# Dense experts of three batches as one chain of 13 tiles, two scan states on the partitions, another stage order

## The chip, the cores and the metric

The kernel runs on one core of one Trainium2 chip, in float32 throughout. The metric is device time in microseconds (us), as the median of several executions; a profile is taken of one further execution. The five engines are TensorE (PE in the rows, its weight loads PEld), VectorE (DVE), ScalarE (ACT), GpSimd (POOL) and SyncE (SP), which only issues transfers.

## The reference, cut to what matters

```python
x = L0_attn_x                                            # 4 batches x 512 tokens x 256 features
x = x + attention(layernorm(x))                          # per token, 16 heads against one key and value
x = x + dense_ffn(layernorm(x))                          # 2 experts, each token takes the likelier (argmax)
    g, u = x @ w_gate[e].T, x @ w_up[e].T                # 1024 wide
    y = (silu(g) * u) @ w_down[e].T * top_w
x = x + state_space(layernorm(x))                        # 8 states for each of 256 features
    x_dbl = x @ W_xproj.T                                # 32 ranks, B (8 states), C (8 states)
    delta = softplus(x_dbl[..., :32] @ W_dt.T + b_dt)
    h[t] = exp(delta * A) * h[t - 1] + (delta * x) * B   # along the 512 tokens
    y = sum over states of h * C, + x * D_param
x = x + sparse_ffn(layernorm(x))                         # top 6 of 64 experts, capacity 64, and a shared expert
```

## The kernel before, in words

Each of the four batches passes through attention, dense experts, the state-space scan and the gate of the sparse experts; then a tail runs all 32 pairs of sparse experts and sums their rows. P is 128, J = 4 tiles of 128 tokens make a batch, K = 2 blocks of 128 features make a row.

What each engine does is cut into stages, such as `ffn.1.3` (batch 1, step 3). One written list, `plan`, gives their order; each engine runs through it (`run`) and executes its own part of those stages that it has a part in, in that order. Nothing overtakes on an engine. Semaphores order the engines among themselves.

**Dense experts.** `route_gate` and `route_slots` norm the tokens, compare the two experts and number the tokens: those of expert 0 from the front, those of expert 1 from the back of 640 slots, so that five tiles (S0 = J + 1) hold a batch whatever the split, each tile of one expert only. GpSimd scatters the rows to `sorted_dram[b]`; SyncE loads them (`ffn_load`), TensorE turns them (`ffn_in`), and each tile takes two halves of 512 (`ffn`: two products of 512 columns for gate and two for up; tanh on ScalarE; `silu` on VectorE; `ffn_h`: four turned blocks) and `ffn_down`. A float32 product appears as two records. `ffn_out` stores the tiles, gathers the rows in token order and adds them. Four batches make 20 tiles, 40 halves.

**Scan.** `ssm_norm`, `ssm_in`, `ssm_proj` give x_dbl, with B and C stored to `bc_dram` and broadcast to all partitions as `bc` (16 rows of 512, 4 MB). `ssm_exp` and `ssm_delta` compute delta; while they run SyncE also issues four clears of `part_rows` (768 KB each, SyncE's `ssm_exp`). A batch has 8 groups: group g holds one block of 128 features on the partitions and two states side by side. For each, ScalarE makes two exponentials (`ssm_a`, line 966), VectorE multiplies (line 1217), scans (line 1221) and multiplies (line 1224), and TensorE adds the two states into `ssm_ps` with the identity (`ssm_sum`, line 728). `ssm_out` turns and adds the result.

**After it.** `gates_in`, `gates`, `places` and `rounds` choose the experts of a batch, `shared_mm`, `shared` and `shared_out` compute the shared expert. These stages of a batch lie among the scan of the next one.

**The start.** The first turn (`attn_turn.0`) waits for all five loads of attention weights, the gate row `g_row` the last of them.

Of the kernel before, what the change touches and what calls it, by code (L numbers as in the profile page):

```python
# [20 lines left out]
F32 = mybir.dt.float32  # L21
# [17 lines left out]
STEPS = S0 * HALF  # L39
# [4 lines left out]
PER_CHUNK = GROUPS // K  # L44
HS_RING = 3
# [23 lines left out]
RT_SEL, RT_DIFF, RT = J + 1, J + 2, J + 11  # L69
# [45 lines left out]
def build(nc, x, wq_t, bq, wkv_t, bkv, gate0, wg0_t, wu0_t, wd0_t, wx_t, wdt_t, b_dt, a_log, d_par,  # L115
          gate1_t, wgu1, wd1, shg_t, shu_t, shd_t, out):
    with ExitStack() as ctx:
# [17 lines left out]
        tile_thr = sb("tile_thr", [1, S0])  # L135
        slot_no = sb("slot_no", [E, CAP])
# [36 lines left out]
        a_col = sb("a_col", [P, K, NS])  # L173
# [23 lines left out]
        rt_ex = sb("rt_ex", [1, B, S0], I32)  # L197
        slot_idx = sb("slot_idx", [P, B, J], U32)
# [15 lines left out]
        bc = sb("bc", [P, 2 * NS, L])  # L214
# [28 lines left out]
        area = bc[:].rearrange("p n l -> p (n l)")  # L243
        at = [0]

        def carve(n):
# [26 lines left out]
        sorted_dram = [nc.dram_tensor(f"sorted_dram{b}", (SLOTS, D), F32).ap() for b in range(B)]  # L273
        ysorted_dram = nc.dram_tensor("ysorted_dram", (SLOTS, D), F32).ap()
# [6 lines left out]
        x_loaded = [sem(f"x_loaded{b}") for b in range(B)]  # L281
        w_attn_loaded = sem("w_attn_loaded")
# [7 lines left out]
        sorted_clear = [sem(f"sorted_clear{b}") for b in range(B)]  # L290
# [27 lines left out]
        du_ready = sem("du_ready")  # L318
        diag_ready = sem("diag_ready")
# [45 lines left out]
            attn_in.0 attn_turn.0 attn_qkv.0.0 attn_in.1 attn_in.2 attn_qkv.0.1 attn_qkv.0.2 ffn_load.0 attn_qkv.0.3  # L365
            attn_score.0 attn_turn.1 attn_add.0 route_gate.0 attn_qkv.1.0 attn_qkv.1.1 attn_qkv.1.2 route_slots.0
            attn_qkv.1.3 attn_score.1 attn_turn.2 attn_add.1 attn_qkv.2.0 ffn_in.0 attn_qkv.2.1 attn_qkv.2.2
            route_gate.1 attn_in.3 attn_qkv.2.3 route_slots.1 ffn.0.0 ffn.0.1 ffn_h.0.0 attn_score.2 ffn.0.2
            ffn_h.0.1 ffn.0.3 ffn_down.0.0 ffn_h.0.2 attn_turn.3 attn_add.2 attn_qkv.3.0 attn_qkv.3.1 route_gate.2
            attn_qkv.3.2 attn_qkv.3.3 ffn.0.4 ffn_h.0.3 route_slots.2 attn_score.3 ffn.0.5 ffn_down.0.1 ffn_h.0.4  # L370
            ffn.0.6 attn_add.3 ffn_h.0.5 ffn.0.7 ffn_down.0.2 ffn_h.0.6 route_gate.3 ffn.0.8 route_slots.3 ffn_h.0.7
# [47 lines left out]
        def run(eng, stages, skips=()):  # L419
# [3 lines left out]
            for name, batch, s in order:  # L423
                for ring, uses, mine in skips:
                    if name not in mine and name in uses:
                        ring.next(uses[name])
# [995 lines left out]
```

## Time and profile before

| | us |
|---|---|
| median of 3 runs | 717.83 (717.29 to 720.01) |
| the profiled execution | 719.09 |
| its span, first to last instruction | 717.4 |
| TensorE busy | 595.6 (83%) |
| VectorE busy | 512.9 (71%) |
| ScalarE busy | 198.1 (28%) |
| GpSimd busy | 104.7 (15%) |
| mean granted TensorE clock | 0.91 of full speed |

A share of the span is a mean over stages with different limits; the rows below cut the span into stages. The profiled execution took 1.7 us more than its span and 1.3 us more than the median.

### The profile page before, as it was taken

Reading aid. Unit: us, or ns where it says so; the run is one execution under the profiler, and the core shown is the slowest. Engines: PE = TensorE matmul, PEld = TensorE weight load, DVE = VectorE, ACT = ScalarE, POOL = GpSimd, SP = SyncE. Lnnn points to the kernel's source line nnn. Section 1 sums busy time; section 2 is a strip of 40 time slices with the busy share of each in tenths; the row PEclk is TensorE's granted clock in tenths of the full one; section 3 lists DMA queues with packets and bytes.
Section 4 is the critical chain, followed back from the end, with each engine's and each line's share of the span. In section 5 each row is a group of like instructions: output and inputs, shape, how many; then the busy total and the mean of one; then the engine's idle time right before and its main releaser. Section 6 shows DMA issues by size and latency. Waiting matters only on the chain.

```text
span 717.4 us, 7176 instructions
## 1 busy us (share of the span) xinstructions
PE 595.6 (83%) x2225; PEld 327.3 (46%) x2225; DVE 512.9 (71%) x1100; ACT 198.1 (28%) x387; POOL 104.7 (15%) x119
## 2 busy tenths in 40 slices
PE   4359998879998869998889988887656699999875
PEld 3235555525555446554355643553243244444554
DVE  7967966155995859997579998699985545555364
ACT  1112221226332334431543232521301133332000
POOL 2022021200002000002000010000000446664200
PEclk9757998998999959999899999999875899999999
DMA  7940000309202192011471010997004579998497
GB/s 276 399 147 32 1 31 15 118 2 359 89 0 67 32 375 80 0 38 30 175 236 37 1 52 16 348 352 230 0 1 164 176 249 364 363 370 294 152 415 290
DMA packets 50371, 114.35 MB, mean 159 GB/s; under 512 B 6112, under 2 KB 32992, under 8 KB 49824
## 3 DMA queue, kind: packets, MB, share of 16 engines
q1 hardware_dynamic: 42576, 94.88, 37.2%
q0 software_dynamic: 5456, 16.91, 6.9%
q10 hardware_dynamic: 2304, 2.10, 0.8%
q8 instruction: 20, 0.33, 0.2%
q14 instruction: 15, 0.12, 0.1%
HBM read 84.26 MB, written 29.62 MB: 159 GB/s over the span
## 4 chain that ended last, share of the span: by engine, by line
PE 49%; DVE 32%; DMA 7%; ACT 5%; issue 4%; SPq 2%; POOL 1%; DVEq 0%; POOLq 0%; ACTq 0%
DVE scan_area L1221 8%; PE gate_ps L808 6%; PE gate_ps L679 6%; PE up_ps L679 6%; PE misc_ps L696 5%; DVE scan_area L1224 4%; DVE scan_area L1217 4%; PE turn_ps L628 4%; DMA bc<-part_rows 3%; PE ssm_ps L728 3%; PE ssm_ps L826 3%; PE misc_ps L826 2%; DVE sig L1161 2%; PE turn_ps L651 2%; PE gate_ps L761 2%
## 5 line engine op out<-in xcount | busy, mean ns | idle before, releaser
L679 PE MATMUL gate_ps<-big,front_area 128*128 x160 | 84.5, 655 | 1.9 <-ACT front_area L866 1.9
L696 PE MATMUL misc_ps<-big,front_area 128*128 x320 | 74.6, 387 | 6.1 <-ACT front_area L866 3.4
L1221 DVE TENSOR_TENSOR_SCAN scan_area<-scan_area 128x1024 f32<-128x1024 f32 x32 | 73.3, 2292 | 7.0 <-ACT scan_area L966 3.4
L679 PE MATMUL up_ps<-big,front_area 128*128 x160 | 77.9, 610 | 0.0
L728 PE MATMUL ssm_ps<-scan_area,ident 128*128 128x512 f32 x128 | 63.3, 629 | 10.6 <-DVE scan_area L1224 9.9
L696 PEld LDWEIGHTS misc_ps<-big,front_area 128*128 128x128 f32 x320 | 61.5, 194 | 23.1 <-issue 15.3
L902 ACT ACTIVATE sig<-gate_ps 128x512 f32<-128x512 f32 (+1 forms) x52 | 30.9, 594 | 104.4 <-PE up_ps L679 67.8
L679 PEld LDWEIGHTS up_ps<-big,front_area 128*128 128x128 f32 x160 | 32.3, 202 | 42.6 <-issue 42.6
L966 ACT ACTIVATE scan_area<-scan_area,a_col 128x511 f32<-128x511 f32 x64 | 42.2, 714 | 33.2 <-DVE scan_area L1221 30.6
L1161 DVE SCALAR_TENSOR_TENSOR sig<-sig,gate_ps 128x512 f32<-128x512 f32 (+1 forms) x52 | 35.5, 682 | 21.5 <-ACT sig L902 14.2
L628 PE MATMUL turn_ps<-ident,front_area 128*128 128x128 f32 x208 | 34.1, 297 | 18.3 <-DMA g_row<-in_gate 10.1
L586 POOL DMA_INDIRECT front_area<-ysorted_dram,slot_idx x16 | 17.3, 1083 | 208.8 <-DMA ysorted_dram<-front_area 205.1
L651 PE MATMUL turn_ps<-w_qkv,front_area 128*128 128x288 f32 x64 | 27.3, 596 | 20.0 <-ACT front_area L866 13.6
L728 PEld LDWEIGHTS ssm_ps<-scan_area,ident 128*128 128x128 f32 x128 | 24.1, 195 | 42.1 <-issue 23.3
L679 PEld LDWEIGHTS gate_ps<-big,front_area 128*128 128x128 f32 x160 | 30.0, 206 | 28.1 <-issue 28.0
L628 PEld LDWEIGHTS turn_ps<-ident,front_area 128*128 128x128 f32 x208 | 26.9, 153 | 34.6 <-issue 21.1
L866 ACT COPY front_area<-turn_ps 128x512 f32<-128x512 f32 (+1 forms) x62 | 34.2, 568 | 24.1 <-PE turn_ps L628 22.7
L1224 DVE TENSOR_TENSOR scan_area<-scan_area,bc 128x1024 f32<-128x1024 f32 x32 | 39.2, 1224 | 1.1
L1217 DVE TENSOR_TENSOR scan_area<-scan_area,bc 128x1024 f32<-128x1024 f32 x32 | 39.0, 1219 | 0.5 <-PE ssm_ps L728 0.2
L611 POOL DMA_INDIRECT part_rows<-bc,att_s x32 | 31.2, 975 | 37.2 <-DVE bc L1352 36.8
L595 POOL DMA_INDIRECT bc<-table,att_s x32 | 30.9, 965 | 27.2 <-DVE att_s L1334 17.7
L1359 DVE SCALAR_TENSOR_TENSOR bc<-bc,gate_ps 128x176 f32<-128x176 f32 x32 | 10.8, 337 | 29.0 <-ACT bc L1011 16.4
(213 smaller groups left out, 887.7 us busy)
## 6 DMA issues: line engine op xcount, KB each, us to landing
bc<-bc_dram SPq DMA_DIRECT2D x4, 4096.0 KB, 13.3
part_rows<-zeros SPq DMA_DIRECT2D x16, 768.0 KB, 15.4
big<-in_wgu SPq DMA_DIRECT2D x15, 704.0 KB
front_area<-in_wgu SPq DMA_DIRECT2D x9, 704.0 KB
big<-part_rows SPq DMA_DIRECT2D x8, 768.0 KB, 10.0
scan_area<-in_wgu SPq DMA_DIRECT2D x6, 704.0 KB
big<-in_wd SPq DMA_DIRECT2D x15, 256.0 KB
front_area<-part_rows SPq DMA_DIRECT2D x5, 768.0 KB, 20.3
```

What stands on the lines that cost most here:

```text
L628: mm = pe.transpose(turn_ps[slot][0:width, col:col + rows], src, ident[0:rows, 0:rows])
L651: mm = pe.matmul(turn_ps[slot][:, 0:QKV], xn_attn_t[:, k, j, :], w_qkv[:, k, :], start=(k == 0), stop=(k == K - 1))
L679: mm = pe.matmul(bank[:], xs_t[:, k, j, :], gu0[:, expert_of[b, j], k, g, half * 512:(half + 1) * 512], start=(k == 0), stop=(k == K - 1))
L696: mm = pe.matmul(misc_ps[:, 0:D], h0_t[:, half, c * P:(c + 1) * P], dn0[:, expert_of[b, j], half * 4 + c, :], start=(half == 0 and c == 0) ...
L728: mm = pe.matmul(ssm_ps[:], ident[:], hs[:, g % HS_RING, n, :], start=False, stop=(g % PER_CHUNK == PER_CHUNK - 1 and n == GROUP - 1))
L808: mm = pe.matmul(gate_ps[p % 2][e * CAP:(e + 1) * CAP, 0:FSH], xg_t[:, p % 2, k, e * CAP:(e + 1) * CAP], gu1[p % RING][:, e * K + k, :], s ...
L826: mm = pe.matmul(y_ps[par][e * CAP:(e + 1) * CAP, 0:D], h1_t[0:rows, par, c, e * CAP:(e + 1) * CAP], dn1[p % RING][c][:, e * D:(e + 1) * D ...
L966: nc.scalar.activation(d_a[:, g % 2, n, 1:L], delta[:, c, 1:L], ACT.Exp, scale=a_col[:, c, n0 + n:n0 + n + 1]).then_inc(da_ready, 1)
L1161: stt(out=s, in0=s, scalar=1.0, in1=gate_ps[slot][0:rows, :], op0=ALU.add, op1=ALU.mult).then_inc(silu_steps, 1)
L1217: tt(buf, sp_z[:, c, :].unsqueeze(1).broadcast_to([P, GROUP, L]), bc[:, n0:n0 + GROUP, :], ALU.mult).then_inc(dbu_ready, 1)
L1221: nc.vector.tensor_tensor_scan(buf.rearrange(flat), d_a[:, g % 2, :, :].rearrange(flat), buf.rearrange(flat), 0.0, ALU.mult, ALU.add).then ...
L1224: tt(buf, buf, bc[:, NS + n0:NS + n0 + GROUP, :], ALU.mult).then_inc(hc_ready, 1)
```

## The change

- **Chain.** Batch 0 keeps its five tiles. Batches 1 to 3 share one array of 13 tiles (`CHAIN`): batch 1 works on five of them, batches 2 and 3 on four each (`TILES_OF`), a tile holding rows of one expert but of several batches. `chain_rows` works out a token's row with 6, 12 and 16 more VectorE instructions for batches 1, 2 and 3. Their loads wait until all four batches' rows are scattered. `ysorted_dram` has an array for batch 0 and one for the chain, of which the rows beyond batch 1's tiles are cleared at the start.
- **States on the partitions.** A group now holds two blocks of 64 features, with state m on partitions 0 to 63 and state m + 4 on 64 to 127. `bc` shrinks to 8 rows, loaded by two transfers of 64 partitions each. delta and delta * x are computed as before and then copied by SyncE into that layout (`spread`, four transfers of 256 KB each, after the clears in its order); ScalarE waits for the first (`delta_spread`), VectorE for the second (`du_spread`). TensorE sums with `fold`, the two halves of the identity added, into 64 partitions of the bank for each of the two blocks. `delta * x` is one instruction of 1024 elements instead of two of 512.
- **First turn.** It waits for the constants only; the first `attn_qkv` waits for the two loads of w_qkv, VectorE for the biases and the gate row.
- **Stage order.** `plan` is rewritten: among others `attn_qkv.2.1` comes ahead of `ffn_in.0`, `attn_add.3` ahead of `ffn.0.6`, `ssm_exp` and `ssm_delta` of batch 1 ahead of `gates.0`, more stages lie between `ssm_delta.b` and `ssm.b.0`, and `weights_more.3` comes before the last batch's routing. An `awake` stage is defined, but the list does not name it.

```diff
+TILES_OF = [S0, S0, J, J]
+TILE_AT = [sum(TILES_OF[0:b]) for b in range(B + 1)]
+CHAIN_AT = [0] + [TILE_AT[b] - S0 for b in range(1, B + 1)]
+CHAIN = (TILE_AT[B] - S0) * P
+Q = P // 2
+BLOCKS = D // Q
+SHARE = NS // 2
+SPREAD = 2 * 2 * 16
-RT_SEL, RT_DIFF, RT = J + 1, J + 2, J + 11
+RT_SEL, RT_DIFF = J + 1, J + 2
+RT_OPS = [J + 11, J + 17, J + 23, J + 27]
...
             def ffn_load(b, _):
-                wait_apart(sp, passed["sp"], (rows_sorted, (B if b % 2 else b + 1) * 16 * J))
+                wait_apart(sp, passed["sp"], (rows_sorted, (B if b else 1) * 16 * J))
...
             def ssm_proj(b, _):
...
-                sp.dma_start(bc[:].rearrange("p n l -> p (n l)"),
-                             bc_dram.rearrange("(o n) l -> o (n l)", o=1).broadcast_to([P, 2 * NS * L])
-                             ).then_inc(bc_loaded, 16)
+                for i in range(2):
+                    sp.dma_start(bc[i * Q:(i + 1) * Q, :, :].rearrange("p (a m) l -> p a (m l)", a=2),
+                                 bc_dram.rearrange("(o a i m) l -> i o a (m l)", o=1, a=2, i=2)[i]
+                                 .broadcast_to([Q, 2, SHARE * L])).then_inc(bc_loaded, 16)
+
+            def spread(wide, narrow, signal):
+                for h in range(2):
+                    for i in range(2):
+                        sp.dma_start(wide[i * Q:(i + 1) * Q, :, :].rearrange("p (c h) l -> p h c l", h=2)[:, h, :, :],
+                                     narrow[h * Q:(h + 1) * Q, :, :]).then_inc(signal, 16)
+
+            def ssm_delta(b, _):
+                wait_apart(sp, passed["sp"], (z_steps, (b + 1) * ZS))
+                spread(delta_wide, delta, delta_spread)
+                wait_apart(sp, passed["sp"], (du_ready, b + 1))
+                spread(du_wide, sp_z, du_spread)
...
             def attn_turn(b, _):
                 if b == 0:
-                    pe.wait_ge(pool_consts, 10)
-                    pe.wait_ge(w_attn_loaded, 16 * 5)
+                    pe.wait_ge(pool_consts, 12)
...
             def ssm_sum(b, g):
...
-                    mm = pe.matmul(ssm_ps[:], ident[:], hs[:, g % HS_RING, n, :], start=False,
-                                   stop=(g % PER_CHUNK == PER_CHUNK - 1 and n == GROUP - 1))
+                    mm = pe.matmul(ssm_ps[n * Q:(n + 1) * Q, :], fold[:], hs[:, g % HS_RING, n, :], start=False,
+                                   stop=(g % PER_CHUNK == PER_CHUNK - 1))
...
             def ssm_a(b, g):
-                    act.wait_ge(z_steps, (b + 1) * ZS)
+                    act.wait_ge(delta_spread, (b + 1) * SPREAD)
...
             def ssm(b, g):
-                c, n0 = g // PER_CHUNK, g % PER_CHUNK * GROUP
+                c, m = g // PER_CHUNK, g % PER_CHUNK
                 if g == 0:
-                    dve.wait_ge(bc_loaded, (b + 1) * 16)
-                if n0 == 0:
-                    dve.wait_ge(z_steps, (b + 1) * ZS)
-                    tt(sp_z[:, c, :], delta[:, c, :], y_fm[:, c, :], ALU.mult).then_inc(du_ready, 1)
-                    dve.wait_ge(du_ready, b * K + c + 1)
+                    dve.wait_ge(bc_loaded, (b + 1) * 32)
+                    dve.wait_ge(du_spread, (b + 1) * SPREAD)
                 wait_from_one(dve, group_summed, at - HS_RING + 1)
-                tt(buf, sp_z[:, c, :].unsqueeze(1).broadcast_to([P, GROUP, L]), bc[:, n0:n0 + GROUP, :], ALU.mult
+                tt(buf, du_wide[:, c * GROUP:(c + 1) * GROUP, :], bc[:, m:m + 1, :].broadcast_to([P, GROUP, L]), ALU.mult
                    ).then_inc(dbu_ready, 1)
```

## Rows read from the trace of the kernel before

**Rows 1.** Busy time of each engine, granted clock and transfers, by stretch.
```profile
core 0: us, PE busy (x) PEld busy (x) DVE busy (x) ACT busy (x) POOL busy (x), PEclk, DMA share, GB/s
...
148.00:238.40 90.40, 83.82 (x267) 45.29 (x266) 64.92 (x82) 33.97 (x57) 3.78 (x4) 0.94 0.29 102
238.40:342.00 103.60, 90.89 (x304) 51.52 (x303) 86.93 (x166) 37.89 (x63) 5.79 (x5) 0.92 0.27 96
342.00:437.70 95.70, 85.42 (x281) 47.80 (x280) 79.94 (x131) 33.73 (x56) 4.71 (x5) 0.95 0.27 97
437.70:532.70 95.00, 74.20 (x215) 38.59 (x213) 83.11 (x150) 27.15 (x41) 1.45 (x1) 0.91 0.52 176
148.00:166.90 18.90, 14.55 (x31) 5.26 (x30) 6.40 (x27) 7.44 (x11) 0.00 (x0) 0.76 0.30 113
179.30:204.00 24.70, 24.59 (x83) 14.31 (x82) 24.02 (x20) 8.14 (x15) 0.00 (x0) 1.00 0.18 65
```

**Rows 2.** VectorE's waits, 148.0 to 532.7: us, times, longest.
```profile
DVE x_res L1311 <- PE misc_ps L779: 7.5, 2, 5.8
...
DVE x_res L1231 <- PE turn_ps L628: 3.7, 1, 3.7
```

**Rows 3.** Instruction groups by shape: busy us, mean ns, idle before.
```profile
L679 PE MATMUL gate_ps<-big,front_area 128*128 x160 | 84.5, 655 | 1.9 <-ACT front_area L866 1.9
L679 PE MATMUL up_ps<-big,front_area 128*128 x160 | 77.9, 610 | 0.0
L696 PE MATMUL misc_ps<-big,front_area 128*128 x320 | 74.6, 387 | 6.1 <-ACT front_area L866 3.4 <-DVE sc L1246 2.6
...
L1161 DVE SCALAR_TENSOR_TENSOR sig<-sig,gate_ps 128x512 f32<-128x512 f32 x48 | 32.8, 683 | 21.5 <-ACT sig L902 14.2 <-issue 6.8
...
L1166 DVE SCALAR_TENSOR_TENSOR front_area<-sig,up_ps 128x512 f32<-128x512 f32 x40 | 27.5, 686 | 1.4
```

**Rows 4.** Start and us: a piece of the chain, a piece of PE's timeline.
```profile
330.02 5.16 PE ssm_ps L728 x12
...
578.50 1.40 PE L808 MATMUL gate_ps<-big,bc 128*64 128x352 f32 x8
```

**Rows 5.** Timeline of batch 0's scan start; then transfers, KB, us to landing.
```profile
160.77 0.33 SPq L492 DMA_DIRECT2D bc<-bc_dram  x1
...
161.14 15.06 SPq L505 DMA_DIRECT2D part_rows<-zeros  x4
...
172.04 1.22 DVE L1204 SCALAR_TENSOR_TENSOR scan_area<-scan_area 128x1024 f32<-128x1024 f32 x1
...
178.54 0.68 DVE L1214 TENSOR_TENSOR scan_area<-scan_area,back_t 128x512 f32<-128x512 f32 x1
...
bc<-bc_dram SPq DMA_DIRECT2D x4, 4096.0 KB, 13.3
...
ysorted_dram<-front_area SPq DMA_DIRECT2D x4, 512.0 KB, 2.9
...
ysorted_dram<-front_area SPq DMA_DIRECT2D x4, 128.0 KB, 1.7
```

**Rows 6.** Timeline: first turn and score, first sorted tiles, routing and load.
```profile
10.07 1.94 PE L628 MATMUL turn_ps<-ident,front_area 128*128 128x128 f32 x8 [10.07 <-DMA g_row<-in_gate]
...
22.27 1.35 DVE L1086 TENSOR_TENSOR xf<-xf,b_qkv 128x1152 f32<-128x1152 f32 x1
...
54.67 2.48 PE L628 MATMUL turn_ps<-ident,front_area 128*128 128x128 f32 x10 [2.72 <-DMA front_area<-sorted_dram]
...
120.30 0.16 DVE L1147 TENSOR_TENSOR rt<-rt 128x4 f32<-128x4 f32 x1
120.50 0.16 DVE L1149 TENSOR_TENSOR rt<-tok_local,rt 128x4 f32<-128x4 f32 x1
...
127.94 0.37 SPq L475 DMA_DIRECT2D front_area<-sorted_dram  x1
...
134.90 1.06 PE L628 MATMUL turn_ps<-ident,front_area 128*128 128x128 f32 x8 [0.91 <-issue]
```

More of the change, by code:

```diff
@@ L68 @@
 AT_DIFF, AT = 5, 10
-RT_SEL, RT_DIFF, RT = J + 1, J + 2, J + 11
+RT_SEL, RT_DIFF = J + 1, J + 2
+RT_OPS = [J + 11, J + 17, J + 23, J + 27]
+RT_AT = [sum(RT_OPS[0:b]) for b in range(B + 1)]
 SOFT_SCALE = 1.89029794104e-5 ** 0.25
@@ L289, in build @@
         scratch_clear = sem("scratch_clear")
-        sorted_clear = [sem(f"sorted_clear{b}") for b in range(B)]
+        sorted_clear = [sem(f"sorted_clear{i}") for i in range(2)]
+        ysorted_clear = sem("ysorted_clear")
         turn_filled = sem("turn_filled")
@@ L364, in build @@
         plan = """
[L365 to L369, printed above, removed]
@@ L400, in build @@
-            shared_mm.3.2 rounds.3.2 tables.3 shared.3.1 shared.3.2"""
+            attn_in.0 attn_turn.0 attn_qkv.0.0 attn_in.1 attn_in.2 attn_qkv.0.1 attn_qkv.0.2 attn_qkv.0.3
+            attn_score.0 attn_turn.1 attn_add.0 route_gate.0 attn_qkv.1.0 attn_qkv.1.1 ffn_load.0 attn_qkv.1.2
+            route_slots.0 attn_qkv.1.3 attn_score.1 attn_turn.2 attn_add.1 attn_qkv.2.0 attn_qkv.2.1 attn_in.3
+            ffn_in.0 attn_qkv.2.2 route_gate.1 ffn.0.0 ffn.0.1 attn_qkv.2.3 route_slots.1 attn_score.2 ffn_h.0.0
@@ L406, in build @@
         order = [(*stage, 0)[0:3] for stage in order]
-        TURNS = dict(attn_turn=2, attn_qkv=1, ffn_in=3, ffn_h=1, ssm_in=2, ssm_out=2, gates_in=2, places=1, tables=1)
+        TURNS = dict(attn_turn=2, attn_qkv=1, ffn_in=(3, 3, 2, 2), ffn_h=1, ssm_in=2, ssm_out=2, gates_in=2, places=1, tables=1)
         MISCS = dict(route_slots=1, ssm_proj=1 + K, gates=1, shared_out=1, ffn_down=1)
@@ L425, in run @@
                     if name not in mine and name in uses:
-                        ring.next(uses[name])
+                        n = uses[name]
+                        ring.next(n[batch] if isinstance(n, tuple) else n)
                 if name in stages:
@@ L639, in turn_tiles, with awake @@
                 pe.wait_ge(turn_moved, turn.so_far())
+            def awake(b, _):
+                if b == 0:
+                    pe.wait_ge(pool_consts, 12)
+                else:
+                    pe.wait_ge(y_moved, B * K)
+                for _ in range(2):
+                    pe.matmul(ssm_ps[:, 0:D], ident[:], zeros[:, 0:D], start=True, stop=True)
             def attn_turn(b, _):
                 if b == 0:
-                    pe.wait_ge(pool_consts, 10)
-                    pe.wait_ge(w_attn_loaded, 16 * 5)
+                    pe.wait_ge(pool_consts, 12)
                 turn_tiles(xn_a[b], J, (0, b))
```

237 lines of the change are left out of this document (161 added, 76 removed).

## The prediction

> **What bounds the kernel now.** I read the stretches of time first, cut where a batch enters its scan (its third layer norm) and where the last batch enters the routing of the sparse experts. From 148.0 to 532.7 us, 384.7 us, neither engine is full: TensorE is busy 83.8 + 90.9 + 85.4 + 74.2 = 334.3 us, VectorE 64.9 + 86.9 + 79.9 + 83.1 = 314.9 us [rows 1]. In the first of these four stages TensorE is 93% busy and VectorE idles 25.5 us; in the last VectorE is 87% busy and TensorE 78%. So the bound passes from TensorE to VectorE inside the stretch that the change works on: TensorE time is worth its price in the first stages and little in the last. When neither waits for the other, VectorE can be packed: 24.02 of 24.70 us between 179.3 and 204.0 [rows 1]. The rest of its idle time is holes, such as the start of a batch's scan (148.0 to 166.9: 6.4 us busy of 18.9) and single waits of 3.7 and 5.8 us for a transposition and for the shared expert [rows 1, 2]. Second, the groups of instructions give the price of each piece; third, the pieces of TensorE's work tell how fast its 64-column form runs; fourth, the start of batch 0's scan and the landings of transfers show what the new transfers will queue behind; last, three places of the front part show what the first turn and the longer routing touch.
>
> **Two tiles fewer.** The dense experts' tiles go from 20 to 18 (5, 5, 4, 4): one less in batches 2 and 3. Per tile TensorE spends (84.5 + 77.9 + 74.6) / 20 = 11.85 us [rows 3], so 23.7 us go (the few turned blocks come on top). VectorE's two halves of SiLU go: 2 x (0.683 + 0.686) = 2.7 us a tile, 5.5 us in all [rows 3]. ScalarE is no bound (at most 38 us of 104 in a stage [rows 1]).
>
> **The sums with 64 columns.** A group's sum is four records of 512 elements into 128 columns; twelve such records take 5.16 us, 1.72 a group [rows 4]. The new form sends each of the two products to its own 64 partitions of the bank. The pairs of sparse experts do the same, eight records of 352 elements in 1.40 us, so four take 0.70, and scaled to 512 elements 1.02 us [rows 4]. At 1.72 us per four records of 512 elements the same eight would have taken 2.37 us; the two halves evidently run beside each other. Saved: 0.70 x 32 groups = 22.4 us. Bounds: nothing (if two products only don't overlap), and 0.86 a group, 27.5 us. I take the nearest row. Together TensorE drops from 334.3 to about 288 us, 75% of the old stretch: VectorE becomes the bound.
>
> **The scan itself.** Multiplication, scan and second multiplication keep their 1024 elements and number, the ScalarE exponentials too; the product of delta and x is one instruction instead of two. Taken as zero on both sides (at most 0.1 us a batch). The sum `fold` is one small instruction, zero.
>
> **The new transfers.** The broadcast of B and C shrinks from 4 MB to two transfers of 1 MB, and eight transfers of 256 KB spread delta and delta*x. The old broadcast lands in 13.3 us, stores of 512 and 128 KB in 2.9 and 1.7 us: 1.3 us fixed and 3.0 to 3.1 us per MB [rows 5]. In SyncE's order the spreads come after the four clears of part_rows (3 MB); its queue was so full that issuing those took 15.06 us [rows 5]. In batch 0 the broadcast goes out at 160.77 and delta is ready at 172.04 + 1.22 = 173.3, 12.5 us later. The new sequence is 2 + 3 + 2 = 7 MB: 1.3 + 21 = 22.3 us after the start, so delta*x is in place 9.8 us after delta, at 183.1; before, the first scan work began at 178.54 [rows 5]. Without the clears in front it would be 1.3 + 6 = 7.3 us. Behind VectorE's wait stand the SiLUs of the next dense halves, and behind ScalarE's wait for the spread delta their tanh, so TensorE would run out of free banks next. The new order puts VectorE work there: two halves of SiLU in batch 0 (2.7 us), and two halves, gating and top-k of an older batch in the others (8 to 9 us with the product itself). I therefore charge about 6 us of new hole in batch 0 and 1 us in each other batch. Behind SyncE's two waits stand the table store of an older batch and the sparse weights, which only the pairs of the tail use: zero, as long as they arrive before them.
>
> Every one of the ten new transfers has only 64 partitions on its SBUF side, and the rows above show none of that form. The Trainium skill speaks against them ("SBUF — State Buffer", Door 1: The DMA port swizzle, and the question on two DMAs that follows): partitions 0 to 63 reach 8 of 16 ports, about 218 GB/s at best, and two transfers on the two halves gain only 6%. By it the 4 MB would take some 19 us instead of 12, 7 us more in each batch and 28 in all, and my sum would end at 719. No row here confirms or denies it; it is a rival below.
>
> **The four stages together.** VectorE's work becomes 314.9 - 5.5 = 309.4 us. Its holes today are 25.5 + 16.7 + 15.8 + 11.9 = 69.8 us [rows 1]. Mine: in the first stage 12.5 (chain before delta, as now) + 6 (spreads) + 2.5 = 21; the others at the level of a stage that is already bound by VectorE, one transposition and one shared-expert wait, 3.7 + 5.8 = 9.5 [rows 2], and half a microsecond for the spreads in the last: 9.5 + 9.5 + 10 = 29. Sum 309.4 + 50 = 359.4 us, that is 25.3 less. Bounds: with holes of 35 us (nearly the packing of the best stretch) 40 us less; with today's 69.8, only 5.5.
>
> **First turn and routing.** The first turn stood until 10.07 us for the gate row, but VectorE is busy with three batches' norms and starts the first attention score only at 22.27 [rows 6]. A turn 1.2 us earlier is hidden behind that: zero; 1.2 us if that cover were gone. Moving attn_qkv.2.1 ahead of ffn_in.0 fills a wait of 2.72 us [rows 6]: -2.7. Against it the chained slot numbers: six, twelve and sixteen more VectorE instructions (after the five that they replace), each 0.16 us and 0.04 of issue [rows 6]: 6.8 us in all, of which only batch 3's last 16, 3.2 us, lie on a path: slot numbers, scatter, load at 127.94, turn at 134.90 [rows 6]. That path starts about 1 us earlier since attn_add.3 comes before a dense half. Net of the front: -2.7 + 3.2 - 1 = -0.5, say 1 us saved; bounds -5 to +2. SyncE's loads of all three chained batches wait for all scatters; batch 1 does so today, and the other two come later anyway. Clearing 18 + 8 tiles instead of 20 lies under 100 us of other work.
>
> **The tail** (routing of batch 3, 32 pairs, sums) keeps its instructions: zero. The sparse weights for the scan area are now asked for before the last routing instead of after it; the pairs run on TensorE's cadence, so nothing is gained.
>
> **Sum.** 719.1 (the profiled execution, span 717.4) - 25.3 - 1 = 692.8; the median of the runs, 717.83, lies 1.3 below that execution, so 691.5, rounded to 691 us.
>
> **Rivals, with chances.**
> *VectorE-bound, as above* (0.60): 679 to 703.
> *Packed better* (0.12): TensorE is now free enough that holes fall to 35 us: 15 us less, about 676 and down to 668. For it: 97% busy between 179.3 and 204.0; against it: each batch still begins with a serial chain.
> *Column halves don't overlap* (0.05): TensorE keeps 22.4 us, has 310.6 against VectorE's 309.4; holes as between today's and mine, 10 us more: 701. Against it the rows of the pairs.
> *The spreads are partly uncovered* (0.10): another 5 or 6 us in each batch, 23 us: 714, at the border of no change.
> *The transfers of 64 partitions run at half the rate* (0.13; the rule of the skill is one road to it): 4 MB at 6 us instead of 3 per MB is 12 us more in each batch. VectorE's filler is used up by the first 9.8 us, so it all shows: 4 x 12 = 48, 739 us. Slower than before from 6.5 us extra a batch on, that is from a rate under two thirds of the broadcast's. For it: half of the partitions; against it: two transfers in a row write different halves, and the queue holds both.
>
> A measurement of this kernel can tell about 0.5% from no change, 3.6 us: 714.2 to 721.4 is "the same". Faster: 0.60 + 0.12 + 0.05 and half of 0.10 = 0.82. Same: 0.05. Slower: 0.13. The range leaves out the half-rate case and the end of the well-packed one: 673 to 718. The likeliest case has 679 to 703.
>
> **What would show it.** Right: 144 gate and 144 up records of the dense halves instead of 160 each [rows 3]; a group's sum near 1.0 us; VectorE's busy time in the scan stretch near 309 us and 85% of it or more; the spreads of delta*x landing 8 to 11 us after delta. Wrong: a long wait of VectorE's first scan multiplication for a transfer (rate), of dense SiLU for tanh with ScalarE standing at the spread delta, four records of a sum still at 1.7 us, or the first turned block of batch 1 after 137 us (the routing chain).

## The result, and the profile after

The changed kernel takes 725.59 us (median of 6 runs, 723.96 to 726.86), the kernel before 718.92 us beside it: a ratio of 1.010, 95% interval 1.007 to 1.014. It is slower by 1.0%. The prediction said 691 us, 673 to 718. Medians here and below are over all runs of a kernel; the ratios leave out executions that lie over 1.5% above the kernel's fastest.

The same cut of the profiled execution (span 723.7) as in [rows 1], with the front part and the tail added; the third layer norm of a batch opens its stage:

```profile
core 0: us, PE busy (x) PEld busy (x) DVE busy (x) ACT busy (x) POOL busy (x), PEclk, DMA share, GB/s
0.00:145.90 145.90, 104.70 (x346) 65.61 (x347) 105.12 (x355) 29.37 (x65) 26.73 (x40) 0.86 0.37 131
145.90:239.80 93.90, 78.33 (x267) 42.62 (x266) 64.55 (x81) 34.51 (x57) 5.49 (x4) 0.91 0.37 97
239.80:340.50 100.70, 79.07 (x257) 40.65 (x256) 82.16 (x145) 33.65 (x55) 6.17 (x5) 0.85 0.35 96
340.50:434.90 94.40, 75.63 (x259) 40.62 (x257) 77.46 (x132) 33.43 (x55) 5.14 (x5) 0.92 0.36 97
434.90:539.80 104.90, 75.23 (x206) 39.05 (x206) 86.62 (x159) 25.85 (x39) 0.39 (x1) 0.75 0.65 192
539.80:723.70 183.90, 151.28 (x811) 76.08 (x811) 97.69 (x253) 34.77 (x104) 62.45 (x65) 0.92 0.72 258
```

The front part ends at 145.9 instead of 148.0 and the tail takes 183.9 instead of 184.7 us. So the loss is all in the four scan stages: 93.9 + 100.7 + 94.4 + 104.9 = 393.9 us against 384.7. VectorE's work there is 310.8 us, TensorE's 308.3 (before: 314.9 and 334.3). Both work less and the stretch is longer. The last digits to read are the granted clock: 0.91, 0.85, 0.92 and 0.75 of full speed, where the same four stages had 0.94, 0.92, 0.95 and 0.91.

The groups of instructions that answer to [rows 3, 4] (busy us, mean ns | idle before it):

```profile
L734 PE MATMUL gate_ps<-big,front_area 128*128 x144 | 75.0, 646 | 1.4 <-ACT front_area L921 1.4
L751 PE MATMUL misc_ps<-big,front_area 128*128 x288 | 74.2, 416 | 9.6 <-ACT front_area L921 8.1 <-DVE sc L1362 1.5
...
L734 PE MATMUL up_ps<-big,front_area 128*128 x144 | 70.4, 613 | 0.0
...
L1333 DVE TENSOR_TENSOR scan_area<-scan_in 128x1024 f32<-128x1024 f32 x32 | 39.1, 1220 | 23.0 <-DMA scan_in<-scan_area 19.0 <-issue 2.4 <-PE ssm_ps L783 1.5
L783 PE MATMUL ssm_ps<-scan_area,fold 128*64 128x512 f32 x128 | 38.1, 696 | 31.1 <-DVE scan_area L1340 30.4 <-ACT front_area L921 0.7
```

144 and 144 records are there instead of 160 and 160, at nearly the old mean (646 and 613 ns, before 655 and 610). The blocks of `ffn_down` (L751) are not cheaper: 288 records take 74.2 us, where 320 took 74.6. The sums of the scan (L783) answer to this row of the kernel before:

```profile
L728 PE MATMUL ssm_ps<-scan_area,ident 128*128 128x512 f32 x128 | 63.3, 629 | 10.6 <-DVE scan_area L1224 9.9 <-ACT front_area L866 0.5
```

They fell from 63.3 us to 38.1. But TensorE now idles 31.1 us ahead of them, where it idled 10.6. And VectorE idles 19.0 us before the scan's first multiplication until a copy lands. Its waits in the four stages:

```profile
DVE sig L1277 <- ACT sig L957: 21.6, 4, 10.3
DVE scan_area L1333 <- DMA scan_in<-scan_area: 19.0, 3, 11.3
DVE scan_area L1312 <- ACT scan_area L1000: 7.1, 1, 7.1
DVE sc_s L1360 <- PE misc_ps L802: 6.2, 1, 6.2
```

The second row is the copies at work. The first, SiLU waiting for tanh up to 10.3 us, looks like the sign that the prediction named for ScalarE standing at the spread delta; a run without the slow copies has to tell (below). Here is the transfer view of batch 3's copies, 471.1 to 482.9 (40 equal slices; DMA is the busy share of the 16 engines in tenths):

```profile
DMA  0000599998998899999999999999999999999999
GB/s 0 0 0 0 125 208 201 215 201 188 222 208 160 243 326 285 222 201 229 201 285 319 271 188 222 222 229 257 222 236 236 215 208 236 220 214 233 363 378 382
DMA packets 1489, 2.53 MB, mean 214 GB/s; under 512 B 128, under 2 KB 465, under 8 KB 1489
...
scan_in<-scan_area SPq DMA_DIRECT2D x8, 256.0 KB, 4.8
```

Nothing else is in flight in front of these eight, and yet 2 MB keep the DMA engines busy for the rest of the 11.8 us: most slices at 0.9 or more, but mostly at 190 to 240 GB/s. The three slices at the end, when the table store and the sparse weights follow, reach 363 to 382. From the first issue of a copy to the first multiplication it is 15.2, 15.7, 11.8 and 11.9 us in the four batches.

### The profile page after: what moved, and what is told of

Its sections match the earlier page's. It is cut to its first block, busy times and chain, and to the rows that moved or that the text cites. A ratio compares the mean times of both kernels' runs of the same rounds, so it can differ in the third digit from the quotient of the medians.

```text
span 723.7 us, 6999 instructions
## 1 busy us (share of the span) xinstructions
PE 564.2 (78%) x2141; PEld 304.6 (42%) x2141; DVE 513.6 (71%) x1123; ACT 191.6 (26%) x375; POOL 106.4 (15%) x120
## 4 chain that ended last, share of the span: by engine, by line
PE 37%; DVE 36%; DMA 10%; SPq 6%; ACT 5%; issue 5%; POOL 1%; DVEq 0%; ACTq 0%; POOLq 0%
DVE scan_area L1337 7%; PE gate_ps L863 6%; PE gate_ps L734 4%; SPq L529 4%; PE misc_ps L751 4%; DMA scan_in<-part_rows 4%; DVE scan_area L1340 4%; PE up_ps L734 3%; DVE scan_area L1333 3%; DMA scan_in<-scan_area 3%; PE ssm_ps L881 3%; PE turn_ps L674 3%; PE misc_ps L881 2%; DVE ln_st L1095 2%; DVE work L1411 2%
## 5 line engine op out<-in xcount | busy, mean ns | idle before, releaser
L751 PE MATMUL misc_ps<-big,front_area 128*128 x288 | 74.2, 416 | 9.6 <-ACT front_area L921 8.1
L734 PE MATMUL gate_ps<-big,front_area 128*128 x144 | 75.0, 646 | 1.4 <-ACT front_area L921 1.4
L751 PEld LDWEIGHTS misc_ps<-big,front_area 128*128 128x128 f32 x288 | 59.6, 210 | 29.1 <-issue 20.2
L734 PE MATMUL up_ps<-big,front_area 128*128 x144 | 70.4, 613 | 0.0
L783 PE MATMUL ssm_ps<-scan_area,fold 128*64 128x512 f32 x128 | 38.1, 696 | 31.1 <-DVE scan_area L1340 30.4
L1021 ACT ACTIVATE scan_area<-scan_in,a_col 128x511 f32<-128x511 f32 x64 | 41.9, 714 | 54.0 <-DVE scan_area L1337 43.0
L1333 DVE TENSOR_TENSOR scan_area<-scan_in 128x1024 f32<-128x1024 f32 x32 | 39.1, 1220 | 23.0 <-DMA scan_in<-scan_area 19.0
L1277 DVE SCALAR_TENSOR_TENSOR sig<-sig,gate_ps 128x512 f32<-128x512 f32 (+1 forms) x48 | 32.8, 683 | 31.1 <-ACT sig L957 31.0
L734 PEld LDWEIGHTS up_ps<-big,front_area 128*128 128x128 f32 x144 | 29.0, 201 | 38.1 <-issue 38.1
L1340 DVE TENSOR_TENSOR scan_area<-scan_area,scan_in 128x1024 f32<-128x1024 f32 x32 | 39.2, 1225 | 1.1
L921 ACT COPY front_area<-turn_ps 128x512 f32<-128x512 f32 (+1 forms) x56 | 31.3, 577 | 30.9 <-PE turn_ps L674 29.6
L657 POOL DMA_INDIRECT part_rows<-scan_in,att_s x32 | 31.2, 974 | 37.7 <-DVE scan_in L1468 36.8
L641 POOL DMA_INDIRECT scan_in<-table,att_s x32 | 30.9, 965 | 26.8 <-DVE att_s L1450 17.4
L783 PEld LDWEIGHTS ssm_ps<-scan_area,fold 128*64 128x64 f32 x128 | 7.5, 148 | 55.3 <-DVE scan_area L1340 42.8
```

What stands on the lines that cost most here:

```text
L734: mm = pe.matmul(bank[:], xs_t[:, k, j, :], gu0[:, expert_of[b, j], k, g, half * 512:(half + 1) * 512], start=(k == 0), stop=(k == K - 1))
L751: mm = pe.matmul(misc_ps[:, 0:D], h0_t[:, half, c * P:(c + 1) * P], dn0[:, expert_of[b, j], half * 4 + c, :], start=(half == 0 and c == 0) ...
L783: mm = pe.matmul(ssm_ps[n * Q:(n + 1) * Q, :], fold[:], hs[:, g % HS_RING, n, :], start=False, stop=(g % PER_CHUNK == PER_CHUNK - 1))
L921: nc.scalar.copy(out_ap, of_bank(turn_ps[slot])).then_inc(turn_moved, 1)
L1021: nc.scalar.activation(d_a[:, g % 2, n, 1:L], delta_wide[:, c * GROUP + n, 1:L], ACT.Exp, scale=a_col[:, c * GROUP + n, m:m + 1]).then_inc ...
L1277: stt(out=s, in0=s, scalar=1.0, in1=gate_ps[slot][0:rows, :], op0=ALU.add, op1=ALU.mult).then_inc(silu_steps, 1)
```

## The experiments

Each ran with the kernel before on the same chip; ratios are to that. All are made from the changed kernel unless said otherwise, and named by their first letters: e1 to e5 and e7 to e16.

### What each part is worth: a square of order and layout

e1 leaves the copies out; e2, e3 and e4 turn the layout, the order or both back.

```diff
 e1:  def ssm_delta(b, _):                  # SyncE: the eight copies go
-         spread(delta_wide, delta, delta_spread)
-         spread(du_wide, sp_z, du_spread)
 e2:  -   d_a ... delta_wide[:, c * GROUP + n, 1:L]     + d_a ... delta[:, c, 1:L]
      -   pe.matmul(ssm_ps[n * Q:(n + 1) * Q], fold[:]  + pe.matmul(ssm_ps[:], ident[:]
 e3:  e2 with the plan of the kernel before, less the ten stages of the two dropped tiles
 e4:  the changed kernel with that plan
```

> The changed kernel without the eight copies of delta and delta * x per batch: ScalarE waits for delta, VectorE for delta * x, and both read the wide area as it was cleared at the start (so the scan's values are left out, its instructions are not). Theory H (holes): the transfers of 64 partitions leave VectorE and ScalarE standing at the start of every scan, some 40 us in four batches (11.3 + 10.3, 5.8, 9.9 + 1.9, 2.4 us of waits); expects 690 to 700 us. Theory O (order and clock): the new stage order, made for other costs, and TensorE's lower clock lose the time; expects 715 to 724.

> The changed kernel with its chain, first turn and stage order, but the scan's layout of before (B and C broadcast as 4 MB, no copies, sums into 128 columns). Theory H: 698 to 708, since VectorE's holes go and TensorE's 25 us more are mostly covered. Theory O: 722 or more, since the order stays and TensorE has more to do.

> Chain of 13 tiles and first turn alone: scan layout and stage order of before, less the ten stages of the two tiles that are gone. 23.7 us of TensorE less than before. Theory H: 700 to 710. Theory O: as low or lower, 697 to 705, and clearly below e2.

> The changed kernel in the stage order of before (less the ten stages): the scan follows delta at once, nothing is put under the copies. Theory H: 732 to 750, since all of the 12 to 15 us from delta to delta * x in place show. Theory O: below 720.

| | median | ratio, 95% interval | scan stages, us |
|---|---|---|---|
| changed kernel | 725.59 | 1.010 (1.007 to 1.014) | 93.9, 100.7, 94.4, 104.9 |
| e1, without the copies | 711.73 | 0.990 (0.984 to 0.995) | 86.7, 95.9, 96.4, 101.4 |
| e2, old layout | 710.51 | 0.989 (0.983 to 0.995) | 87.2, 92.8, 96.9, 102.3 |
| e3, old layout and order | 712.36 | 0.992 (0.988 to 0.997) | 90.4, 93.7, 96.0, 97.7 |
| e4, old order | 756.12 | 1.051 (1.044 to 1.057) | 100.2, 103.8, 109.1, 107.4 |

Three things follow. The chain (with the first turn) is worth 8 us by itself, although it takes 24 us of work from TensorE. The layout loses 44 us in the old order and 15 in the new: the new order hides 29 us of what the copies' delay costs, which is what it is good for; with the old layout the two orders can't be told apart (710.5 and 712.4 us, while e3's runs spread from 709.0 to 718.8). And without any copy the new layout is no faster than the old one (711.7 to 710.5), although its sums take 28 us less of TensorE. In e4, where the scan follows delta at once, less of the copies' delay is covered: VectorE waits 34.8 us for them instead of 19.0. Its waits over the span:

```profile
DVE scan_area L1333 <- DMA scan_in<-scan_area: 34.8, 4, 13.2
...
DVE scan_area L1312 <- ACT scan_area L1000: 19.8, 3, 11.8
```

### Why the copies are slow: the form of the transfer

```diff
 e11: - two broadcasts of 64 partitions, four copies of 64 partitions for each array
      + sp.dma_start(bc ..., bc_dram ...[0:1].broadcast_to([P, 2, SHARE * L]))
      + for h in range(2): sp.dma_start(wide ...[:, h, :, :], narrow)      # 128 partitions
 e7:  + sp.dma_start(wide_dram[at], narrow); then for c, h:
      + sp.dma_start(wide[:, 2 * c + h, :], wide_dram[at][h * Q:(h + 1) * Q, c, :]
      +              .unsqueeze(0).broadcast_to([2, Q, L]))                # B and C alike
 e8:  the copies of delta * x issued by ScalarE (act.dma_start) ahead of its wait for delta's
```

> The changed kernel with the same bytes moved to the same tiles, but in transfers that write 128 partitions from sources that stand right: B and C as one broadcast of 2 MB (the upper 64 partitions get the lower ones' states), delta and delta*x as two copies of 512 KB each from 128 partitions to 128 (the blocks that a partition gets are not those of the reference). So no work is left out, only the values differ. Theory 1 (a transfer of 64 partitions moves at half the rate): B and C land 6 to 8 us after the first issue instead of 12.2, the four copies 6.5 to 8.5 us after theirs instead of 11.8 to 15.7, the waits of line 1333 for a transfer fall from 19.0 us to under 8 and the time to 712 to 719 us. Theory 2 (bytes alone count): 12 us and 11 us again and 722 to 728 us.

Measured: 711.09 us (708.54 to 712.47), 0.988 (0.981 to 0.995). The broadcast of 2 MB lands in batch 0 after 8.5 us instead of 12.2. The copies are all there 7.9 us after the first issue in batch 0 and at most 7.4 us in batch 3 (2.3 us for the issues, 5.1 to landing), instead of 15.2 and 11.9. The transfer view from batch 3's first copy on, 461.5 to 471.0:

```profile
DMA  0000019999999999999999999999999999989998
GB/s 0 0 0 0 0 60 388 379 371 354 388 371 362 405 354 388 371 397 405 345 371 397 405 362 397 336 345 397 371 355 372 356 329 259 167 189 183 199 172 183
DMA packets 1580, 2.73 MB, mean 287 GB/s; under 512 B 64, under 2 KB 556, under 8 KB 1580
...
scan_in<-scan_area SPq DMA_DIRECT2D x4, 512.0 KB, 4.2
```

The same 2 MB and the same engines, as busy as before, but mostly 350 to 400 GB/s instead of 190 to 240; the slices at the end are other transfers. Besides the partitions, e11 changes the number of copies (four instead of eight) and their size (512 KB instead of 256). The size alone does not explain the rate: in the changed kernel the two broadcasts of 1 MB, each into 64 partitions, take 12.2 us too. VectorE waits for a transfer once, 4.1 us in batch 0, instead of three times and 19.0 us. The longest waits in the scan stages are now:

```profile
DVE sig L1274 <- ACT sig L954: 23.4, 5, 11.4
DVE scan_area L1309 <- ACT scan_area L997: 7.1, 1, 7.1
...
DVE sc_s L1357 <- PE misc_ps L799: 6.2, 1, 6.2
```

So the long waits of SiLU (L1274), of the softplus (L1309) and of the sparse gate (L1357) are not the copies': they are up to 11.4, 7.1 and 6.2 us here too. The longest, in order of time:

```profile
353.70 0.69 DVE L1274 SCALAR_TENSOR_TENSOR sig<-sig,gate_ps 128x512 f32<-128x512 f32 x1 [11.37 <-ACT sig L954]
```

Batch 2's norm began at 329.1. TensorE turns and projects it, ScalarE computes its exponentials and tanh, and the tanh of a dense half is queued behind them; VectorE stands for 11.37 us. The time of e11 equals that of e1, without copies (711.1 and 711.7 us): at full rate they cost nothing that can be told, in half rows they cost 14.5 us. The Trainium skill ("SBUF — State Buffer", Door 1: The DMA port swizzle) says that 64 partitions reach half the ports; the trace agrees with some 220 against 360 GB/s.

> The changed kernel, but every transfer of the scan's inputs writes 128 partitions: B and C as two transfers of 1 MB, and delta and delta*x stored to memory (512 KB each) and read back as four transfers of 256 KB each over 128 partitions. In the changed kernel 2 MB take 12.2 us for B and C and 11.8 us for the copies, each transfer touching 64 partitions on the receiving side. Theory 1 (a transfer of 64 partitions moves at half the rate of one of 128): B and C land within 6 to 8 us of their first issue, and the eight loads of the copies take 7 to 9 us from their first issue, with a store of about 3 us ahead of them, so that the first multiplication comes 10 to 13 us after the first issue: 717 to 726 us. Theory 2 (the rate goes by the bytes written, the same for both forms): B and C still take 12 us, the copies 12 us and the store in front of them, so 728 to 736 us. The Trainium skill (page SBUF, the section on the DMA port swizzle) states a rule that would make theory 1 true.

Measured: 990.96 us, ratio 1.379. Neither theory: this kernel tests something else. One window between 208 and 233 us, when only the loads run, and the issue of those loads:

```profile
208.00:233.00 25.00, 0.00 (x0) 0.00 (x0) 0.00 (x0) 1.31 (x3) 0.00 (x0) 0.50 0.13 48
```

```profile
L531 SPq DMA_DIRECT2D scan_in<-wide_dram x32: 501/5040/7292, 208.2 to 724.5; - x32
```

DMA share 0.13 is as much as two of the sixteen engines fully busy (0.13 x 16 = 2.1), at 48 GB/s. These transfers have an outermost dimension of 2 on their source side (the two halves of the partitions); that this is why so few engines work is my reading, since no run changes it alone. One issue holds SyncE 5.0 us in the median. So the run says nothing about half rows. e11, whose outermost dimension is 128, asks the question without that.

> The changed kernel, with the four copies of delta*x issued by ScalarE, which stands waiting for delta's copies at that point, and no longer by SyncE behind delta's. SyncE needs 7.5 to 10.0 us to issue eight copies. Theory 1 (the ports of 64 partitions bound the 2 MB): the last copy still lands 11 to 12 us after the first issue in batches 2 and 3, and the time is 723 to 727 us. Theory 2 (one queue's issue and its order bound it): the last copy lands 7 to 9 us after the first issue, the wait of line 1333 nearly vanishes (19.0 us to under 6) and the time falls to 712 to 719 us.

Measured: one execution of 725.69 us and three of 738.2 to 738.6 (median 738.33). Even the shortest equals the changed kernel. The trace is of an execution of 738.43 us, so only its transfers are read here:

```profile
L1012 ACTq DMA_DIRECT2D scan_in<-scan_area x16: 597/1410/2287, 172.5 to 481.5; - x16
...
DMA to landing us min/median/max: 5.4/7.4/11.7
```

ScalarE needs 1.4 us in the median for the issue of a copy (SyncE 1.0 in the changed kernel), and the tanh of the experts stands behind it in its order. In batch 3 the first copy is issued at 476.6 and the last at 481.5, and none of ScalarE's lands in less than 5.4 us: 2 MB still need at least 10.3 us, as theory 1 has it. The 7 to 9 us of theory 2, and its gain, did not come. What it does to the waits this run can't tell.

### What stands in front of the copies

The clears are issued in all four batches of the changed kernel, not only in the first two, as the next expectation has it. In batches 0 and 1 the issue of the last clear ends 1.6 and 1.3 us before the first copy, in batches 2 and 3 some 7 and 9 us before it.

```diff
 e5:  SyncE's four clears of part_rows leave ssm_exp and follow the copies in ssm_delta
 e16: the same on top of e11
```

> The changed kernel, with the clears of part_rows (four 768 KB stores in the first two batches' stages) issued by SyncE after the eight copies of delta and delta*x and no longer ahead of them. In the changed kernel the first multiplication of the scan starts 15.2 and 15.7 us after the first issue of a copy in batches 0 and 1, where clears stand ahead, and 11.8 and 11.9 us in batches 2 and 3, where the queue is empty. If the clears are what stretches the first two, both fall to about 12 us, the waits of line 1333 for a transfer (19.0 us in all) to about 11, and the time by 4 to 8 us, to 718 to 722 us. If the copies only share SyncE's slow issue (7.5 to 10 us for eight), the first two starts stay over 14 us and the time within 2 us of 725.6.

Measured: 714.29 us (10 runs), 0.994 (0.991 to 0.996). The first multiplication comes 11.6 and 11.5 us after the first issue in batches 0 and 1, and the waits for a transfer fall to 11.2 us, as expected; the gain of 11 us is more than the 4 to 8 expected. The granted clock of the scan stretch is 0.87 instead of 0.85; that this is the rest of the gain was not tested.

> The experiment with full-row transfers (711.1 us; the same bytes as the changed kernel, values differ) and the clears behind the copies as well. With clears ahead its four copies landed 4.6 us (median) after issue. Theory 1 (the clears cost only together with half-rate copies; behind full-rate ones nothing waits): 709 to 713 us. Theory 2 (a gain of its own, as the 11 us of the fifth experiment): 700 to 706 us.

Measured: 710.82 us, 0.991 (0.987 to 0.994), against 711.09 for e11. Theory 1: the clears have no price of their own that can be told once the copies go in full rows.

### Why TensorE's saved work is not seen

```diff
 e9:  e1, and - tt(buf, buf, bc[:, SHARE + m ...], ALU.mult)     # VectorE's multiplication by C
 e10: e1, and + for _ in range(4): pe.matmul(ssm_ps[:, 0:D], zeros[:, 0:P], zeros[:, 0:D])
 e13: e2, and the same four ahead of each group sum
```

> The changed kernel without the copies of delta and delta*x (as in the first experiment, 711.7 us) and, besides, without VectorE's second multiplication in the scan, the one by C: 32 operations of 1.22 us, 39.1 us of VectorE's work, are left out, so the sums add states that were not multiplied. TensorE's and ScalarE's work stays. Theory 1 (VectorE sets these stages, as the prediction had it: work plus a fixed hole): the time falls by 30 to 39 us, to 673 to 682 us. Theory 2 (the stages run by chains through TensorE and ScalarE at the granted clock, and VectorE's share is only one of several): it falls by 8 to 20 us, to 692 to 704 us. Under 5 us would say that VectorE has slack all through.

> The changed kernel without the copies of delta and delta*x (711.7 us), and with four matmuls of zero weights over 256 columns added ahead of each of the 32 group sums, while TensorE waits for the group: about 128 x 0.25 us = 32 us of work more. In the first experiment TensorE did 25 us less than in the old layout and the granted clock between 340 and 530 us was 0.80 against 0.86, at the same end. Theory 1 (the saved work is paid back by the clock): the clock of that stretch rises to 0.88 or more, each gate matmul becomes shorter, and the time falls or stays, 703 to 712 us, for 32 us of added work. Theory 2 (TensorE's order of work carries the stages and the clock follows for other reasons): the added work shows in the time, 716 to 730 us.

> The second experiment (chain of 13 tiles, first turn and new order with the old scan layout, 710.5 us) with the same filler as the run beside it: four matmuls of zero weights over 256 columns ahead of each of the 32 group sums, about 32 us of TensorE's work. TensorE is busier here than without copies. If slack of TensorE is what the two tiles left behind, the time stays within 4 us (707 to 714 us); if TensorE's order carries the stages, it rises by 8 to 25 us, to 718 to 735 us.

The four scan stages as one window of each, e2, e1, e9, e10 and e13 in this order (PE busy, PEld busy, DVE busy, ACT busy, POOL busy; clock; DMA):

```profile
145.10:524.30 379.20, 318.51 (x986) 175.85 (x984) 311.43 (x520) 127.63 (x206) 17.89 (x15) 0.91 0.36 125
```
```profile
146.00:526.40 380.40, 308.73 (x986) 165.29 (x984) 310.70 (x517) 127.47 (x206) 18.15 (x15) 0.85 0.35 104
```
```profile
144.00:509.80 365.80, 302.84 (x984) 161.49 (x983) 274.01 (x485) 127.44 (x206) 16.93 (x15) 0.86 0.36 109
```
```profile
147.00:539.00 392.00, 344.44 (x1242) 201.33 (x1240) 310.93 (x517) 126.88 (x206) 16.18 (x15) 0.94 0.34 104
```
```profile
146.10:553.00 406.90, 362.77 (x1242) 221.68 (x1240) 311.97 (x520) 127.20 (x206) 15.69 (x15) 0.94 0.34 119
```

e9: 699.03 us (690.36 to 701.33), 0.967 (0.958 to 0.976). 36.7 us less of VectorE's work shorten the stretch by 14.6 and the time by 12.7 us. VectorE alone does not set these stages. e10: 727.33 us, 1.011 (0.999 to 1.022): 35.7 us more of TensorE's work, at a clock of 0.94 instead of 0.85, lengthen the stretch by 11.6 us and the median by 15.6, with a wide scatter (721.2 to 734.8); part of it filled the wait ahead of the sums (23.4 us in e1, 3.7 here). e13: 740.1 us, 1.031 (1.023 to 1.039): 44.3 us more lengthen the stretch by 27.7 and the median by 29.6. So a microsecond added to TensorE shows 0.3 to 0.7 of itself, and one taken from VectorE 0.35 to 0.40. Theory 2 of e9 and e10 holds, and the last expectation's second theory in kind; its upper end, 735 us, was too low, and the added work was more than the 32 us I had set. VectorE's holes are no fixed sum either: stretch less VectorE's work is 69.7 us in e1, 91.8 in e9, 81.1 in e10 and 94.9 in e13. These are prices of adding to TensorE; they don't prove what removing its work brings.

That is seen between e2 and e1. The group rows of both:

```profile
L716 PE MATMUL gate_ps<-big,front_area 128*128 x144 | 72.9, 631 | 1.4 <-ACT front_area L903 1.4
...
L765 PE MATMUL ssm_ps<-scan_area,ident 128*128 128x512 f32 x128 | 64.3, 638 | 16.1 <-DVE scan_area L1322 15.2 <-ACT front_area L903 0.7
...
L816 PE MATMUL misc_ps<-w_shd,hsh_t 128*128 128x256 f32 (+1 forms) x72 | 21.7, 462 | 5.4 <-DVE x_res L1409 2.4 <-DVE hsh_t L1264 2.0 <-DVE sc L1344 1.1
```

```profile
L729 PE MATMUL gate_ps<-big,front_area 128*128 x144 | 74.5, 644 | 1.4 <-ACT front_area L916 1.4
...
L778 PE MATMUL ssm_ps<-scan_area,fold 128*64 128x512 f32 x128 | 36.2, 670 | 23.4 <-DVE scan_area L1336 22.7 <-ACT front_area L916 0.7
...
L829 PE MATMUL misc_ps<-w_shd,hsh_t 128*128 128x256 f32 (+1 forms) x72 | 24.8, 515 | 5.3 <-DVE hsh_t L1278 2.2 <-DVE x_res L1423 2.0 <-DVE sc L1358 1.1
```

The sums lost 28.1 us of busy time (64.3 to 36.2), but TensorE's total in the stretch only 9.8 (318.51 to 308.73). Of the other 18.3 us 15.8 are longer matmuls of the same number and shape: without the sums, the groups of the stretch add up to 278.7 us in e2 and 294.5 in e1. The remaining 2.5 us are less overlap between groups. The granted clock fell from 0.91 to 0.85, most visibly in some small products: the shared expert's second product (L816, L829) went from 462 to 515 ns, a gate product only from 631 to 644. With the filler of e10, at a clock of 0.94, the same product is short again:

```profile
L831 PE MATMUL misc_ps<-w_shd,hsh_t 128*128 128x256 f32 (+1 forms) x72 | 21.2, 454 | 7.9 <-DVE x_res L1425 4.3 <-DVE hsh_t L1280 2.5 <-DVE sc L1360 1.1
```

And what was left turned into a wait for VectorE's groups, 16.1 to 23.4 us.

### The other parts

> The kernel before, with only the first turn's edit: TensorE's first transposes no longer wait for the attention's weights, which get a semaphore of their own ahead of the first projection. The prediction costs this edit at nothing: first score at the same time within 0.5 us, the time within 2 us of the kernel before. The rival is that it brings or costs 2 to 4 us by what it does to the clock at the start or to the order of batch 0.

```diff
 e12 (kernel before): - pe.wait_ge(w_attn_loaded, 16 * 5)   # first turn
                      + pe.wait_ge(w_qkv_loaded, 16 * 2)    # first attn_qkv
```

Measured: 721.34 us against 717.02, ratio 1.002 (0.997 to 1.006): no difference that can be told, as predicted.

```diff
 e14 (e2), e15 (e5): the stages behind ssm_norm.3 in the order of the kernel before
```

> The second experiment (chain of 13 tiles, first turn, old scan layout, new order; 710.5 us) with the stages behind ssm_norm.3 in the order of the kernel before (one stage, rounds.1.2, stands there in addition). The last scan stage took 102.3 us in the second experiment, 97.7 us in the third (old order throughout), 95.0 us in the kernel before. Theory 1 (the new order's tail of the plan costs it): the stage falls to 96 to 99 us and the time to 704 to 708 us, the fastest version so far. Theory 2 (the length comes from what the new order leaves over from earlier stages, or from the lower clock): 709 to 713 us.

Measured: 706.87 us (705.77 to 707.56, 6 runs), 0.985 (0.981 to 0.989), the fastest version here that leaves no work out. Its last scan stage and that of e2:

```profile
423.20:521.70 98.50, 74.41 (x206) 39.24 (x206) 86.73 (x161) 26.06 (x39) 1.45 (x1) 0.84 0.49 170
```

```profile
422.00:524.30 102.30, 77.26 (x206) 41.64 (x206) 86.84 (x161) 25.86 (x39) 0.39 (x1) 0.82 0.56 192
```

The same work, 98.5 instead of 102.3 us: the new order's last part costs 3.8 us in this layout.

> The fifth experiment (changed kernel with late clears, 714.3 us) with the same change of the last stage's order. Its last stage is 104.7 us. Theory 1: it falls by 3 to 6 us, to 708 to 712 us. Theory 2: 713 to 717 us.

Measured: 718.58 us (713.91 to 719.89, 11 runs), 1.001 (0.998 to 1.004); the profiled execution has a last stage of 108.4 us instead of 104.7. Both theories miss. In the new layout the old tail leaves less other work over batch 3's copies: VectorE waits 8.4 us for them ahead of that batch's first multiplication, where in e5 it stood 2.2 us.

## Why the prediction was wrong

- **The price of the copies** is the first failed step: "1.3 us fixed and 3.0 to 3.1 us per MB", taken from transfers over all 128 partitions for transfers over 64. Measured, 2 MB take 11.8 us with nothing in front: less 1.3, that is 5.3 us per MB. The text charged 6 + 1 + 1 + 1 us of new holes, but the sum took in only 6 and half a microsecond; measured, the copies' form costs 14.5 us of time (e11 against the changed kernel; e1 says 13.9). The rival had the mechanism right, but I priced it at 48 us and gave it 0.13. 48 was too much: the new order's other work hides part of each delay. The 44 us of the old order (e4 against e3) lie near 48, but they are the cost of the whole layout, not only of the slower rate. The sum by the rule of the Trainium skill ("SBUF — State Buffer", Door 1: The DMA port swizzle), 719, lies nearer to the result than mine, by luck: its 28 us for the copies are twice what they cost, and that covers part of the holes below.
- **The holes** are the second and larger one: "the others at the level of a stage that is already bound by VectorE", 50 us in all. VectorE's work of 309.4 us was right (310.8). With the copies at full rate (e11) its holes are 380.4 - 310.8 = 69.6 us; before they were 69.8. In sum they did not shrink. Nor did they in e1 (69.7), e2 (67.8) and e3 (68.1), whatever the layout and the order. The stages of e11:

```profile
146.50:233.20 86.70, 76.09 (x266) 42.35 (x265) 64.53 (x80) 34.48 (x57) 5.50 (x4) 0.94 0.31 105
233.20:329.10 95.90, 78.95 (x256) 41.23 (x255) 82.21 (x146) 33.71 (x56) 6.18 (x5) 0.86 0.30 101
329.10:425.50 96.40, 79.40 (x260) 42.60 (x258) 77.51 (x133) 33.53 (x55) 6.70 (x5) 0.87 0.28 95
425.50:526.90 101.40, 74.21 (x206) 38.95 (x206) 86.51 (x160) 25.85 (x39) 0.39 (x1) 0.76 0.58 199
```

  The holes are 22.2, 13.7, 18.9 and 14.9 us, where I set 21, 9.5, 9.5 and 10. The bound that I had written down, "with today's 69.8, only 5.5", is what happened: the stretch of e11 is 4.3 us shorter than before. Of the signs that I had named, the long wait of SiLU for tanh came, but not from the copies. The longest single holes are the chain from a batch's norm to its delta, which I had charged in the first stage only (12.5 us). In e11 it makes VectorE wait 10.4, 7.1 and 11.4 us in the first three stages. Before, it did so too, seen at the softplus (12.1 and 6.1 us the longest):

```profile
DVE scan_area L1195 <- ACT scan_area L945: 19.1, 3, 12.1
...
DVE sig L1161 <- ACT sig L902: 4.6, 4, 2.6
```

  The new order moved the wait and did not shorten it: the softplus waits 7.1 us instead of 19.1, and SiLU 23.4 instead of 4.6. In the last stage it is another one: 6.2 us for TensorE's scores of the sparse gate and 4.1 for the shared expert. The level of 9.5 us that I gave the others is one transposition and one wait for the shared expert; it holds nothing for this chain, which the second and third stage have. TensorE's free time did not shorten it; why not is shown only in part (the next point).
- **TensorE's saving** failed as a term: 334.3 - 23.7 - 22.4 would be 288 us; it is 308.3. The column halves did what was said (a group's sum 1.19 us busy, from 1.98: 25.2 us less, where 22.4 were forecast), and the two tiles are gone. Most of the 20 us came back in longer matmuls, at a granted clock of 0.85 instead of 0.93 over the stretch: the projection to delta, for one, takes 813 ns instead of 689. Some 3 us by my estimate are the edge of the stretch, which has 14 gate and 12 up records fewer than before and not 16 each. I had held the durations of TensorE's instructions as fixed.
- **The copies' place in the queue** was right in direction: behind the clears they take 15.2 and 15.7 us, in front of them 11.6 and 11.5.
- **Tail and front** were right: 183.9 for 184.7 and 145.9 for a predicted 147.0; batch 1's first turn comes at 134.24, before the 137 that would have shown the routing chain as the cause; the first turn brings nothing that can be told (e12).

The account of the profiled spans: predicted 717.4 - 26.3 = 691.1, measured 723.7, that is 32.6 us apart. Front and tail give -1.9; the copies' form 13.5 (stretch 393.9 against 380.4 in e11); and e11 is 21.0 us over my 359.4: 19.6 of holes that stayed (69.6 - 50) and 1.4 of VectorE's work. Of the 21.0, 3.8 belong to the order of the last stage, if e14's gain holds in this layout, which e15 does not confirm. Where exactly the clock's loss and the three engines' mutual waits divide the rest, these runs leave open.

## What to carry to other kernels

When a change gives one engine less work, ask of each hole what ends it before shrinking it: here the prediction took 46 us from TensorE, the trace shows 26, and VectorE's holes stayed at 70 us. Price a transfer by a row of its own form; the number of partitions it writes is part of the form, by e7 perhaps its outermost dimension too, and where no row has it, the rival with the other rate deserves more than a small chance. An order of stages made for a long transfer hid two thirds of its cost here (44 us to 15); what the transfer's removal brings is then the rest and not its length.

## What the runs showed of the hardware

- With 28 us of TensorE's sums less the mean granted clock (its levels are 1.2 and 2.4 GHz) fell from 0.91 to 0.85 in the scan stages (e2, e1), and the other matmuls took 16 us longer; with the gaps filled by idle products it was 0.94 (e10).
- 64-partition copies moved at some 220 GB/s with the DMA engines busy 0.9 of the time; full rows at some 360.
- Transfers with an outermost dimension of 2 on the source side kept the DMA engines busy for a share of 0.13, as much as two of sixteen, at 48 GB/s, with 5.0 us in the median for an issue (e7).
- The issue of one 64-partition copy of 256 KB took 0.6 to 2.2 us on SyncE and 0.6 to 2.3 on ScalarE (e8); eight of them held SyncE for 7.5 to 10 us.
